# Transformer block on one core: the feed-forward stage's opening moved about among the last attention units

## The reference, cut to what matters

```python
h = _rmsnorm(x, g1) * (1.0 + scale1[:, None, :]) + shift1[:, None, :]
x = x + _mha(h, w_qkv, b_qkv, w_ao, b_ao, n_head)      # softmax(q k^T / sqrt(hd)) v, then @ w_ao + b_ao
h = _rmsnorm(x, g2) * (1.0 + scale2[:, None, :]) + shift2[:, None, :]
x = x + _ffn(h, w_fc, b_fc, w_fo, b_fo)                # (a * silu(gate)) @ w_fo + b_fo, a and gate from h @ w_fc
```

## Time and profile before

| | us |
|---|---|
| median of three runs | 3267.48 (3260.66 to 3269.02) |
| the profiled execution: its own time | 3263.67 |
| its span in the profile | 3261.9 |
| PE busy | 3083.3 (95%) |
| DVE busy | 1876.9 (58%) |
| ACT busy | 1518.4 (47%) |
| POOL busy | 1717.1 (53%) |

### The profile page before, as it was taken

How to read it: one execution, slowest core, us unless ns; L and a number is a source line. 1 busy time by engine, 2 the same in 40 slices (tenths; PEclk the granted TensorE clock), 3 DMA queues, 4 the chain that set the end, 5 groups by cost and what they waited for, 6 DMA issues and landing times.

```text
span 3261.9 us, 39659 instructions
## 1 busy us (share of the span) xinstructions
PE 3083.3 (95%) x15073; PEld 2088.2 (64%) x15073; DVE 1876.9 (58%) x2979; ACT 1518.4 (47%) x2791; POOL 1717.1 (53%) x737
## 2 busy tenths in 40 slices
PE   6996889999999999999999988799999999999999
PEld 6775665555555555555555544478888888888887
DVE  3665768787877888787787867443333333222222
ACT  2222237676767777676676756532322222111111
POOL 3453458888888888887888977632222210000000
PEclk9898999999999999999999989899999999999999
DMA  4455459899898998989889897732223201122110
GB/s 174 152 171 149 138 139 197 177 203 189 183 199 177 201 195 186 201 178 186 188 185 207 177 200 163 161 94 79 84 77 95 86 1 58 52 78 78 52 52 26
DMA packets 170638, 456.14 MB, mean 140 GB/s; under 512 B 23873, under 2 KB 57745, under 8 KB 138641
## 3 DMA queue, kind: packets, MB, share of 16 engines
q0 software_dynamic: 32256, 234.90, 36.2%
q1 hardware_dynamic: 136368, 213.21, 22.3%
q10 hardware_dynamic: 1824, 5.51, 0.4%
HBM read 140.03 MB, written 78.64 MB: 67 GB/s over the span
## 4 chain that ended last, share of the span: by engine, by line
PE 44%; POOL 22%; DMA 20%; issue 9%; DVE 3%; ACT 1%; SPq 1%; POOLq 0%; DVEq 0%; ACTq 0%
DMA b_pt<-b_pt 17%; POOL b_acc L802 16%; PE e_g L1413 10%; PE e_a L1413 10%; PE e_y L1423 10%; POOL b_acc L790 3%; PE b_s L887 3%; PE b_o L935 2%; PE e_p L1358 2%; PE b_m L871 2%; POOL a_q_lo L313 2%; PE a_qk L470 1%; POOL a_yq L306 1%; DMA b_qs<-scratch_qk_lo 1%; PE a_c L438 1%
## 5 line engine op out<-in xcount | busy, mean ns | idle before, releaser
L819 DVE TENSOR_REDUCE b_mpart<-b_m 128x1 f32<-128x512 f32 x1960 | 1200.2, 680 | 327.0 <-PE b_m L871 327.0
L770 ACT ACTIVATE b_pt<-b_s 128x512 f32<-128x512 f32 x2048 | 1088.9, 601 | 425.3 <-PE b_s L887 381.0
L802 POOL TENSOR_TENSOR b_acc<-b_acc,b_pt 128x2048 f32<-128x2048 f32 x224 | 1042.8, 4655 | 205.4 <-DMA b_pt<-b_pt 204.6
L887 PE MATMUL b_s<-b_qs,b_ks 98*128 98x512 f32 x2048 | 857.4, 421 | 57.2 <-ACT b_pt L770 33.3
L871 PE MATMUL b_m<-b_ks,b_qs 96*128 96x512 f32 x1960 | 760.2, 408 | 0.0
L887 PEld LDWEIGHTS b_s<-b_qs,b_ks 98*128 98x128 f32 x2048 | 392.0, 192 | 385.3 <-issue 191.0
L935 PE MATMUL b_o<-b_pt,b_vg 128*32 128x512 f32 x4096 | 504.0, 610 | 0.0
L871 PEld LDWEIGHTS b_m<-b_ks,b_qs 96*128 96x128 f32 x1960 | 375.2, 191 | 126.6 <-DVE b_mpart L819 54.2
L1297 DVE SCALAR_TENSOR_TENSOR e_u_lo_f<-e_a,keep_chan,e_u_lo_f 128x512 f32<-128x512 f32 x128 | 96.0, 750 | 539.0 <-PE e_a L1413 539.0
L1413 PE MATMUL e_g<-e_h_hi,e_w 128*128 128x512 f32 x1024 | 340.7, 394 | 27.9 <-DVE e_w_lo L1289 19.8
L1413 PE MATMUL e_a<-e_h_hi,e_w 128*128 128x512 f32 x1024 | 337.8, 391 | 0.0
(11 more groups left out here) (131 smaller groups left out, 3054.7 us busy)
## 6 DMA issues: line engine op xcount, KB each, us to landing
b_pt<-b_pt POOLq DMA_DIRECT2D x224, 1024.0 KB, 8.2
scratch_qk_hi<-a_q_hi SPq DMA_DIRECT2D x64, 256.0 KB
scratch_qk_lo<-a_q_lo SPq DMA_DIRECT2D x64, 256.0 KB
b_qs<-scratch_qk_hi SPq DMA_DIRECT2D x64, 256.0 KB, 6.8
b_ks<-scratch_qk_hi SPq DMA_DIRECT2D x32, 512.0 KB, 6.6
scratch_v<-a_vsb SPq DMA_DIRECT2D x32, 256.0 KB, 2.6
b_qs<-scratch_qk_lo SPq DMA_DIRECT2D x32, 256.0 KB, 9.7
b_ks<-scratch_qk_lo SPq DMA_DIRECT2D x16, 512.0 KB, 8.6
```

What stands on the lines that cost most here:

```text
L770: act.activation(pt[:, kt % RING, h, :], ps_s[:, score_place(i) % LEAD, :], ACT.Exp, scale=SCALE).then_inc(p_ready, 1)
L802: pool.tensor_tensor(acc[u % 2][:], acc[u % 2][:], pt[:, (2 * n + 3) % RING, :, :], ALU.add).then_inc(pool_added, 1)
L819: dve.tensor_reduce(mpart[n % 2][:, i // 4, i % 4:i % 4 + 1], ps_m[:, at, :], AX.X, ALU.max).then_inc(max_done, 1)
L887: pe.matmul(ps_s[:, place % LEAD, :], ks[n // NJ % 2][0:QR, h, kt * P:(kt + 1) * P], qs[n % 4][0:QR, h, :], start=True, stop=True).then_in ...
```

## The change

It touches the head and the first tile of stage e:

- **Loads.** `head_sync` is called three times a unit. The four loads (attention products and reciprocals, `x`, `w_ao`) that stood together at the end of unit 28 are spread: products and reciprocals over unit 28, `w_ao` and `x` over unit 29, first weight blocks at the ends of 29 and the start of 30, biases and second weight blocks in unit 30.
- **VectorE.** The four products `e_oa_f` go from unit 30 to unit 29; the `_lo` parts go from the second call of unit 30 to the first; rounding `wo_hi` goes to ScalarE (four activations in unit 30) with the roundings of `e_ob` from steps 12 to 15 to steps 0 to 3. Scaling the rows of tile 0 goes from ScalarE to VectorE, the transposes come one step sooner, and weight block 0 is rounded at step 12 of unit 31.
- **Weights.** The two weights of a block have semaphores of their own: `w1_ready` for `hidden`, `w_ready` for `project`. Only two blocks are split before the first tile, block 2 after the first gate, block 3 after the second and before ScalarE's `round_output`. SP loads tile 1's products right behind block 2, and tile 1's `x` behind block 3.
- **GpSimd.** The last two sums of unit 31 stand behind tile 1's `take_in` and `add_first`, tile 0's `add_second` behind both. The last `denominators` goes from behind f = 1 to behind f = 3. `d_sb`, `dcol`, `junk` lie elsewhere.

```diff
     for u in range(UNITS):
...
             load_piece(u, 0)
+            head["sync"](sp, u, 0)
             sp.wait_ge(pv_done, NK * u + RING - 1 + 6)
             load_piece(u, 1)
+            head["sync"](sp, u, 1)
...
-            head["sync"](sp, u)
+            head["sync"](sp, u, 2)
...
+    def head_sync(sp, u, step):
+        at = 3 * (u - HOME) + step
+        if at == 0:
+            b["outputs_stored"](sp, u, u - 1)
+            load_products(sp, 0)
+        if at == 1:
+            load_reciprocals(sp, 0)
+        if at == 3:
+            sp.dma_start(wo_f[:], io["w_ao"].rearrange("(k p) n -> p k n", p=P)).then_inc(wo_in, 16)
+        if at == 4:
             load_x(sp, 0)
+        if at in (5, 6):
+            load_first(sp, at - 5)
...
         for n in range(2, NF):
             load_weights(n)
-            if n == 3:
+            if n == 2:
                 sp.wait_ge(xT_done, KT)
                 load_outputs(sp, 1)
+            if n == 3:
+                sp.wait_ge(b["st_done"], STEPS * (UNITS + 1))
+                load_x(sp, 1)
...
     def head_vector(dve, u, late):
-        if u == LAST - 1 and late:
-            dve.wait_ge(wo_in, 16)
-            dve.tensor_copy(wo_hi[:], wo_f[:]).then_inc(wohi_done, 1)
+        if u == LAST - 2:
             dve.wait_ge(o_in, 16 * (GH + 1))
-            for k in range(KT):
+            for k in ((0, 1), (2, 3))[late]:
                 dve.tensor_tensor(oa_f[:, k, :], oa_f[:, k, :], ob_f[:, k, :], ALU.mult).then_inc(on_ready, 1)
+        if u == LAST - 1 and not late:
             for k in range(KT):
                 dve.wait_ge(ohi_ready, k + 1)
                 dve.tensor_tensor(oa[:, k, :], oa_f[:, k, :], f32(ob[:, k, :]), ALU.subtract).then_inc(olo_ready, 1)
+            for k in range(KT):
+                dve.wait_ge(wohi_done, k + 1)
+                dve.tensor_tensor(wo_lo[:, k, :], wo_f[:, k, :], f32(wo_hi[:, k, :]), ALU.subtract).then_inc(wo_ready, 1)
...
+            dve.wait_ge(rstd_ready, 1)
+            for i in range(SUB):
+                dve.tensor_scalar(oa_f[:, i, :], y[0][:, i, :], rs[:, i:i + 1], None, ALU.mult).then_inc(xn_done, 1)
...
     def head_scalar(act, u, kt):
-        if u == LAST - 1 and kt >= NK - KT:
-            round_output(act, 0, kt - NK + KT)
+        if u == LAST - 1:
+            if kt < KT:
+                round_output(act, 0, kt)
+            elif kt < 2 * KT:
+                act.wait_ge(wo_in, 16)
+                act.activation(wo_hi[:, kt - KT, :], wo_f[:, kt - KT, :], ACT.Copy).then_inc(wohi_done, 1)
...
         for c in range(1, TILES):
-            normalise(c)
+            take_in(c)
+            if c == 1:
+                b["gpsimd_late"](pool, 0)
+            round_off(c)
             add_first(c)
+            if c == 1:
+                b["gpsimd_late"](pool, 1)
+                add_second(0)
             add_second(c)
```

More of the change, by code:

```diff
@@ L778, in scalar_tail, with add_pair, gpsimd_late @@
         read_denominators(act, UNITS)
+    def add_pair(pool, u, n):
+        pair_landed(pool, u, n)
+        pool.wait_ge(pool_added, added(u, n) - 1)
+        pool.tensor_tensor(acc[u % 2][:], acc[u % 2][:], pt[:, (2 * n + 3) % RING, :, :], ALU.add).then_inc(pool_added, 1)
+    def gpsimd_late(pool, k):
+        if k:
+            pool.sem_inc(pool_added, 1)
+        add_pair(pool, UNITS - 1, PAIRS - 2 + k)
     def gpsimd(pool, stage_a):
@@ L1183, in round_u @@
             act.activation(u_hi[:, f % 2, :], u_f[:, f % 2, :], ACT.Copy).then_inc(uhi_ready, 1)
-        for n in range(3):
-            split(n)
+        round_first(act, 1)
+        for n in range(2):
+            round_second(act, n)
         gate(0, 0, 0)
         round_u(0, 0)
+        split(2)
         for q in range(TILES):
@@ L1209, in scalar @@
                 round_u(nq, nf)
+                if q == 0 and f == 0:
+                    split(3)
                 if more and f == 0:
@@ L1216, in scalar @@
                     round_h(act, c, 2 * (f - T_AT) + 1)
-                if q == 0 and f + 3 < NF:
+                if q == 0 and 0 < f < NF - 3:
                     split(f + 3)
@@ L1304, in finish @@
                 dve.tensor_tensor(y[c % 2][:, i, :], ps_y[:, i, :], y[c % 2][:, i, :], ALU.add).then_inc(y_done, 1)
-        for n in range(3):
-            split(n)
+        lo_first(dve, 1)
+        for n in range(2):
+            lo_second(dve, n)
         value(0, 0, 0)
+        split(2)
         for q in range(TILES):
@@ L1379, in head_turned @@
     def head_turned(pe, u, kt):
-        if u == LAST and kt in (13, 14):
+        if u == LAST and kt in (12, 13):
             pe.wait_ge(xn_done, SUB)
-            for k in (2 * kt - 26, 2 * kt - 25):
+            for k in (2 * kt - 24, 2 * kt - 23):
                 pe.wait_ge(x2_ready, k + 1)
@@ L1391, in attention_out @@
             pe.wait_ge(olo_ready, KT * (c + 1))
-            if c == 1 and i == 0:
+            if c == 2 and i == 0:
                 pe.wait_ge(b["d_read"], UNITS + 2)
@@ L1415, in hidden, with project @@
             last.then_inc(done, 1)
-        def project(q, f):
+        def project(q, f, half):
             pe.wait_ge(ulo_ready, NF * q + f + 1)
+            pe.wait_ge(w_ready, NF * half + f + 1)
             if f == 0:
```

110 lines of the change are left out of this document (54 added, 56 removed).

## The result

| | before | changed |
|---|---|---|
| median, first comparison | 3268.25 us (4 runs) | 3248.22 us (4 runs, 3246.13 to 3248.81) |
| ratio, 95% interval | | 0.9942, 0.9925 to 0.996 |
| median, repeated on another chip | 3259.12 us (17 runs, 3250.2 to 3281.64) | 3255.42 us (12 runs, 3246.44 to 3262.41) |
| ratio, 95% interval | | 0.9982, 0.9963 to 1.0 |
| the profiled execution: time, span | 3263.67, 3261.9 us | 3248.63, 3246.8 us |

The first comparison makes the changed kernel 0.6% faster; the second says 0.2%, with an interval that reaches 1.0. Executions of this kernel differ by more than the change brings, and between the two profiled executions of the changed kernel the difference lies ahead of the change.

A forecast was written before the change was run, and what follows sets the result against it. TensorE, busy 95% of the span, was taken as the bound, so only its idle time could be won. The terms summed to -27.0 us, from the profiled execution's 3263.7 to 3236.7, stated as 3237 us, range 3222 to 3252.

The forecast's parts named there:

- queries, unit 29: Unit 29: TensorE's 14.6 us wait for unit 31's queries goes, and a slow start of 1.9 with it: -16.5 us.
- exponentials, unit 30: Unit 30: two pairs of value products take 10.9 us instead of 20.9, without the wait for exponentials: -10.0 us.
- ScalarE's eight activations: Unit 30's first eight steps: eight added activations cost between 0 and 5.1 us, given slack: +1.2 us.
- products on VectorE: End of unit 29: GpSimd's sums hold VectorE's products, TensorE waits for maxima: +4.0 us (0.5 to 5.5).
- `_lo` parts: Unit 30: eight subtractions need gaps between GpSimd's sums, unit 31's first projection waits: +4.0 us (0 to 8).
- loads: Units 28 to 30: the head loads now spread there cost +2.0 us (0 to 8.7).
- unit 31, the rest: Unit 31: row scaling leaves ScalarE, one weight rounding comes in: -0.7 us (-2.5 to +2).
- start of stage e: After attention: TensorE starts sooner, with a new wait of about 7 us before tile 1's projection: -11.0 us (-18 to -7).
- The rival that it gave 0.04: Units 28 to 30: DMA time is the true price of the head loads; about 3270 us, chance 0.04.
- What would show it wrong: Attention ending less than 8 us sooner, or `e_p` starting later than 50 us after attention's last matmul.
- VectorE becomes the bound: Units 29 to 31: VectorE's terms at upper ends, `x` adds unfinished at ScalarE's squares; about 3251 us, chance 0.12.
- The head loads still collide, now with unit 30's maxima and the ring: Head loads give back a wait of 14 us; 3256 us and above, chance 0.06.

The follow-up runs named there:

- Experiment 4: Changed kernel with GpSimd's first late sum behind tile 1's `_lo` parts instead of ahead of them; 3246.88 us (one run).
- experiment 3: Changed kernel with unit 31's first projection waiting for its operands quarter by quarter, not for all eight; 3260.01 us (one run).
- Experiment 1: Changed kernel without VectorE's four products at the end of unit 29, only the semaphore raised; 3247.09 us (one run).
- Experiment 2: Changed kernel with the loads of `w_ao` and `x` moved to the end of unit 29; 3253.0 us (one run).
- experiment 8: Experiment 4's kernel with the reciprocals' load moved from unit 28's second step to its end; 3251.43 us (one run).
- 9: Changed kernel with the edits of experiment 4, experiment 7 and experiment 8 together, products on VectorE; 3231.66 us (6 runs), 0.9917 of before.
- 10: Kernel 9 with the four products on GpSimd, two behind each of its first two adding transfers of unit 30; 3241.09 us (11 runs).
- 12: Kernel 9 measured again, beside the changed kernel on one chip; 3233.22 us (6 runs), 0.9921 of before.
- experiment 5: Kernel before, with unit 31's queries issued ahead of the head's 4 MB of loads, nothing else changed; 3257.6 us (one run).
- experiment 7: Experiment 4's kernel with unit 31's first projection waiting by quarters and ScalarE's squares at steps 5 to 8; 3243.64 us (one run).

## Why the prediction was right, and where not

It said 3237 us, 27 less, in 3222 to 3252. The direction was right. The first comparison, 3248.22, lies in the range; the repetition, 3255.42, lies above it. The profile gives 11.5 us of gain where 27.0 were written, and the first comparison's 20.0 us hold more than that, so that 3248.22 lies in the range is in part luck. By the prediction's own terms:

| term | predicted | measured | read from |
|---|---|---|---|
| queries, unit 29 | -16.5 | -16.4 | pair 22.69 to 6.33 |
| exponentials, unit 30 | -10.0 | -9.3 | pair 14.73 to 5.43 |
| ScalarE's eight activations | +1.2 | +0.3 | three pairs of 5.93 to 5.95 |
| products on VectorE | +4.0 | +10.6 | pair 16.60 less 5.99 |
| `_lo` parts | +4.0 | +3.7 | unit 31's first pair |
| loads | +2.0 | +7.4 | unit 29's third and fourth pairs |
| unit 31, the rest | -0.7 | +1.2 | last pair of 30, rest of 31 |
| start of stage e | -11.0 | -9.0 | E to the end |
| sum | -27.0 | -11.5 | |

In the changed kernel's second execution products read +10.9, `_lo` parts +4.9, loads +8.2 and the rest of unit 31 -1.5, so single terms move by up to 3 us.

**Right.** Both stalls that it said would go are gone, at the size it gave. The start of stage e came as worked out to within a microsecond: first `e_g` at E + 4.4 (E + 4.4), tile 1's data at E + 21.6 (E + 22.6), `e_p` at E + 39.45 (E + 38.9), and 7.5 us of new wait (7). Experiment 4 shows its cause, the one late sum. 11.1 us were won up to `e_p`, whose first matmul before starts at 2134.79, E + 50.5, a little ahead of the row that the prediction read; of the 2.1 given back behind it the prediction had 0.9, for TensorE's last sums; 1.2 I did not follow. The `_lo` parts were done at 2021.8, 20.7 us after step 10 of unit 30 began (about 20), and experiment 3 shows that the first projection's wait was theirs.

**Products on VectorE: the step that failed most, in size.** The step "7 to 8 us late, and has about 1.2 us of slack per pair" was nearly right for each pair: 5.41 and 5.00 us, 10.4 where 2.4 would do, so 8.0 late. What failed was what that costs. The prediction let four maxima banks and the slack take 3 to 4 of the 8. They took 1: TensorE waited 2.73 + 4.32 = 7.05 us for maxima. And its pair was 10.6 too long, in part because it also ran slow: the granted clock is 1.00 up to 1963.2, 0.81 over the 3.0 us of work behind the first wait, and 0.50 in and behind the second. There the distance from one matmul to the next is 0.43 us instead of 0.23; the eight from 1970.52 to 1974.23 took 3.7 us instead of 1.9. The upper bound, 5.5, was too low: it let the slack take most of the delay and had no slow clock. Experiment 1 settles the cause: without products, 0.4 us are lost at the border.

**Loads: sized too low.** 7.4 instead of 2.0, though within its upper bound of 8.7. The prediction priced them by keys, 2.9 us for 1.5 MB in unit 25, and then took less still, because VectorE's waits would give the queues time. Experiment 2 clears most of `w_ao` and `x`, and 8, 9, 10 and 12 put 4 to 6 of the 7.4 us on the reciprocals where they were. The rival that it gave 0.04 had a price for broadcast loads, 13 us a MB from tile 1's reciprocals; for this one load of 1 MB that is twice what it cost or more. The loss shows half a unit after its cause. GpSimd's sum waits 4.98 us for its transfer in unit 28, with the products' load under way (experiment 8), and the reciprocals add to it. GpSimd does not catch up, since a sum and an issue fill 4.57 + 0.88 of a pair's 5.83 us, and one more late transfer in unit 29 (4.15) is followed by the wait that TensorE sees. How the loss of 1.5 to 3.6 us that is left in 8, 9, 10 and 12 is shared between the products' load and this transfer is not shown.

**What would show it wrong** was "attention ends less than 8 us sooner (some unit has a new wait of its own)". Behind S it ended 2.5 us sooner, and the new waits are in units 29 to 31. By its own criterion the working was wrong about attention, though the time was in range. The nearest of its rivals is "VectorE becomes the bound" (about 3251, 0.12), but it came only in part: the products went over their upper end (10.6, 5.5), the `_lo` parts did not (3.7, 8), and ScalarE's squares, which it also had, waited only in experiments 2, 3, 8 and 12. It deserved more than 0.12. Its argument against, that GpSimd runs dry when TensorE stalls, holds for the sum at 1972.46 and comes too late: the stall is the cost.

"The head loads still collide, now with unit 30's maxima and the ring" was given 0.06. The changed kernel shows the ring's part of it, and experiment 5 the other: 5.73 us of wait for maxima that go through memory behind 4 MB.

## What to carry to other kernels

When a stall is removed, list what ran inside it. In the kernel before, VectorE's four products stood in the stall of unit 30 and took 2.48 us, while GpSimd waited for value products:

```profile
2015.91 2.48 DVE L1259 TENSOR_TENSOR e_oa_f<-e_oa_f,e_ob_f 128x512 f32<-128x512 f32 x4
```

```profile
2023.26 0.87 POOL L796 DMA_DIRECT2D b_pt<-b_pt  x1 [8.37 <-PE b_o L935]
```

Among the sums of unit 29 the same four took 10.4. Move first the work that stands in a critical engine's queue behind such an operation, then the stall: experiment 3 took the wait away alone and got it back one pair later, experiment 7 moved ScalarE's squares as well and kept the gain. Look for the cost of a load where the next engine runs out of slack, here half a unit on. And when executions vary by more than the change is worth, measure from a point just ahead of the change within each profile, and profile one kernel twice to see how much that stretch varies.
